# Bias rows in the routing, keys ahead of queries, and new orders in attention, in a fused cross-attention and mixture-of-experts kernel

## The reference, cut to what matters

```
x = x + attention(layernorm(x), ctx, ctx)        # scores / 4, causal mask, softmax, times values
h = layernorm(x)                                 # 1024 tokens x 256
logits = h @ router_weight.T + router_bias
top_val, top_idx = top_k(logits, 4); scores = softmax(top_val) placed at top_idx, else 0
gate, up = split(h @ gate_up_proj[e] + gate_up_bias[e])      # min(gate, 7), clip(up, -7, 7)
out_e = ((up + 1) * gate * sigmoid(1.702 * gate)) @ down_proj[e] + down_bias[e]
x = x + sum_e scores[:, e] * out_e
```

## Time and profile before

| what | us |
|---|---|
| median of 3 runs | 311.38 |
| the profiled execution | 311.51 |
| its span, first to last instruction | 309.8 |
| attention, to the last copy of `o_t` (L706) | 0 to 106.9 |
| routing, to the first L1535 | 106.9 to 134.7 |
| block loop, to the end of the last L1535 | 134.7 to 286.6 |
| last stage | 286.6 to 309.8 |
| PE busy in the span | 268.6 (87%) |
| DVE busy | 183.5 (59%) |
| ACT, POOL busy | 159.1, 159.0 (51% each) |

### The profile page before, as it was taken

One profiled execution on the slowest core, in us unless ns is written; L12 is line 12 of the kernel. 1 busy time (PEld: TensorE's weight loads), 2 busy tenths in 40 slices (PEclk: granted clock), 3 DMA queues, 4 the chain that ended last, 5 costly groups with the idle time before them and its releaser, 6 DMA issues.

```text
span 309.8 us, 5662 instructions
## 1 busy us (share of the span) xinstructions
PE 268.6 (87%) x1517; PEld 175.4 (57%) x1523; DVE 183.5 (59%) x479; ACT 159.1 (51%) x361; POOL 159.0 (51%) x225
## 2 busy tenths in 40 slices
PE   7796897699799625779999989999998989998994
PEld 7764565376577414435655655666655656555673
DVE  3897746944868787535535545555544546654495
ACT  3334655335465437646557556676755755654200
POOL 6871815712535777253566656666557565553000
PEclk9799999959999955899999999999999999999759
DMA  7605050043059999154232222222232222331693
GB/s 249 231 3 190 19 204 3 1 156 119 2 194 355 413 412 372 43 159 167 81 104 74 87 72 88 88 90 88 75 85 87 85 91 72 82 83 47 234 329 135
DMA packets 26494, 42.35 MB, mean 137 GB/s; under 512 B 2688, under 2 KB 19168, under 8 KB 26208
## 3 DMA queue, kind: packets, MB, share of 16 engines
q1 hardware_dynamic: 21776, 29.27, 26.3%
q0 software_dynamic: 4416, 12.45, 13.2%
q10 hardware_dynamic: 272, 0.26, 0.3%
HBM read 29.66 MB, written 12.26 MB: 135 GB/s over the span
## 4 chain that ended last, share of the span: by engine, by line
PE 71%; DVE 12%; issue 4%; ACT 4%; DMA 3%; another core or an unknown queue 2%; POOL 1%; SPq 1%; ACTq 0%; DVEq 0%
PE ps L1535 27%; PE ps L1554 13%; DVE neg_max L897 6%; PE ps L1266 5%; PE ps L1544 4%; PE ps L1582 3%; PE ps L1518 3%; PE ps L1342 3%; PE ps L1318 2%; PE ps L1285 2%; PE ps L1569 2%; DMA br_sb<-n_L_ffn_router_bias_dram 2%; PE ps L1371 1%; DVE x_tok L929 1%
## 5 line engine op out<-in xcount | busy, mean ns | idle before, releaser
L1535 PE MATMUL ps<-w_all,q_norm 128*128 x188 | 90.4, 603 | 5.1 <-issue 2.6
L648 POOL DMA_INDIRECT pair_rows<-y_ext,slot_row x45 | 45.5, 1010 | 51.9 <-ACT y_ext L830 38.9
L1174 DVE TENSOR_SCALAR v_aug<-ps 128x256 f32<-128x256 f32 x47 | 20.0, 425 | 69.0 <-PE ps L1535 49.0
L642 POOL DMA_INDIRECT ctx_tok<-y_rows,slot_tok x47 | 46.0, 979 | 21.3 <-issue 14.0
L1535 PEld LDWEIGHTS ps<-w_all,q_norm 128*128 128x128 f32 x188 | 32.0, 190 | 32.0 <-issue 31.8
L1554 PEld LDWEIGHTS ps<-w_all,o_t 128*128 128x128 f32 x188 | 35.3, 190 | 25.8 <-issue 23.3
L1554 PE MATMUL ps<-w_all,o_t 128*128 x188 | 48.6, 381 | 1.1 <-ACT o_t L821 1.1
L557 POOL TENSOR_SCALAR_AFFINE_SELECT w_all<-w_all 128x256 f32<-128x256 f32 (+1 forms) x48 | 23.1, 500 | 41.6 <-ACT w_all L698 40.8
L816 ACT ACTIVATE v_aug<-v_aug 128x256 f32<-128x256 f32 x47 | 19.6, 417 | 46.1 <-DVE v_aug L1174 39.2
L698 ACT ACTIVATE w_all<-ps 128x512 f32<-128x512 f32 x48 | 25.7, 599 | 24.1 <-PE ps L1318 24.1
L897 DVE TENSOR_REDUCE neg_max<-ps 128x2 f32<-128x512 f32 (+1 forms) x48 | 30.5, 685 | 8.0 <-PE ps L1291 5.5
(11 more groups left out here) (161 smaller groups left out, 389.0 us busy)
## 6 DMA issues: line engine op xcount, KB each, us to landing
w_all<-_L_ffn_gate_up_proj_dram SPq DMA_DIRECT2D x16, 512.0 KB, 5.8
w_all<-in_L_ffn_down_proj_dram SPq DMA_DIRECT2D x16, 256.0 KB, 6.5
pair_rows<-zeros SPq DMA_DIRECT2D x4, 1024.0 KB, 4.5
bias_all<-n_gate_up_proj_bias_dram SPq DMA_DIRECT2D x2, 2048.0 KB, 12.4
w_all<-pair_rows SPq DMA_DIRECT2D x8, 512.0 KB, 6.6
x_tok<-in_x_dram SPq DMA_DIRECT2D x4, 256.0 KB, 4.4
out_dram<-x_tok SPq DMA_DIRECT2D x4, 256.0 KB, 2.1
ctx_tok<-in_ctx_dram SPq DMA_DIRECT2D x3, 256.0 KB, 5.3
```

The costliest lines, as they stand in the source:

```text
L642: pool.indirect_dma_start(out=xg[:, i % XG, :], out_offset=None, in_=y_dram[:, :], in_offset=bass.IndirectOffsetOnAxis(ap=slot_tok[:, i:i ...
L648: pool.indirect_dma_start(out=pair_dram[:, :], out_offset=bass.IndirectOffsetOnAxis(ap=slot_row[:, i:i + 1], axis=0), in_=o_sb[:, i % O_RI ...
L1535: mm = pe.matmul(o, x_t[:, i % 3, k, :], w_all[:, bass.ds(e, 1), k * 2 * F:(k + 1) * 2 * F].rearrange("p a n -> p (a n)"), start=False, st ...
```

## The change

- In attention, `stack_low` and `dup` do the keys before they wait for the queries.
- M of batch 0's first half comes before its last four X steps, and `slot(0)` and `slot(1)` are written anew.
- The statistics of batches 2 and 3 move from the start into `slot(0)`, their powers behind masks; `x1_rows(0)` moves from the middle of `slot(1)` to behind M(2, 1), and `tokens(0)` from the end of `slot(1)` into `slot(2)`.
- PE turns the router's weights just before M(0, 0).
- The routing scores are turned in two halves. The bias rows are made in the routing, in banks 0, 1, 4 and 5, and DVE adds them onto `x_tok` (x1) there: batches 0 and 1 between `router_scores(2)` and `places(2)`, 2 and 3 behind `slot_tokens`. `open_banks` and the eight fill matmuls are gone, and four stand ahead of the last two batches' bias rows.
- In the last stage no bias rows are made. `planes_of` also adds x1 onto the planes, and `last_sum` opens its banks itself.

```diff
 def slot(b):
+    if b == 0:
+        order = [("T", new, (0, 1, 2)), ("S", b, (0,)), ("M", b, (1,)), ("S", b, (1,)),
+                 ("T", new, (3, 4, 5)), ("S", b, (2,)), ("T", new, (6,)), ("X", new, (0, 1)), ("T", new, (7,)),
+                 ("X", new, (2, 3)), ("S", b, (3,)), ("X", new, (4, 5)), ("S", b, (4,)), ("X", new, (6, 7)),
+                 ("V", b, (0,)), ("M", new, (0,)), ("X", new, (8, 9)), ("V", b, (1,)), ("X", new, (10, 11)),
+                 ("S", b, (5,)), ("V", b, (2, 3)), ("M", new, (1,))]
+    if b == 1:
+        order = [("T", new, (0, 1, 2)), ("V", old, (4,)), ("T", new, (3, 4, 5)), ("V", old, (5,)),
+                 ("S", b, (0,)), ("V", old, (6,)), ("T", new, (6,)), ("V", old, (7,)),
+                 ("X", new, (0, 1)), ("S", b, (1,)), ("X", new, (2, 3)), ("S", b, (2,)),
+                 ("X", new, (4, 5)), ("S", b, (3,)), ("O", old, (0, 1)), ("T", new, (7,)), ("S", b, (4,)),
+                 ("X", new, (6, 7)), ("V", b, (0,)), ("M", new, (0,)), ("X", new, (8, 9)),
+                 ("V", b, (1,)), ("X", new, (10, 11)), ("S", b, (5,)), ("V", b, (2, 3)),
+                 ("M", new, (1,))]
...
 first = (("T", (0, 1, 2, 3, 4, 5)), ("X", (0, 1)), ("T", (6,)), ("X", (2, 3)), ("T", (7,)),
-         ("X", (4, 5, 6, 7, 8, 9, 10, 11)), ("M", (0,)))
+         ("X", (4, 5, 6, 7)), ("M", (0,)), ("X", (8, 9, 10, 11)))
...
 def stack_low(eng, b):
-    eng.wait_ge(stack_hi, 2 * b + 2)
-    eng.wait_ge(q_norm_ready, TB * (b + 1))
+    eng.wait_ge(stack_hi, 2 * b + 1)
     eng.tensor_tensor(ks[:, :, 48:64], src_k, ks[:, :, 0:16].bitcast(F32), ALU.subtract).then_inc(stack_lo, 1)
+    eng.wait_ge(stack_hi, 2 * b + 2)
+    eng.wait_ge(q_norm_ready, TB * (b + 1))
     eng.tensor_tensor(qs[:, :, 16:32], src_q, qs[:, :, 0:16].bitcast(F32), ALU.subtract).then_inc(stack_lo, 1)
...
 def row_bank(b):
-    return (0, 1, 0, 5)[b]
+    return (0, 1, 4, 5)[b]
...
 # POOL
-            for b in range(1, B):
-                rsqrt(b, 0)
+            rsqrt(1, 0)
...
                     select(u + 1)
-                    if n == (1 if b == B - 1 else 4) and b >= 1:
-                        rsqrt(b - 1, 1)
+                    if b == 0 and n in (1, 4):
+                        rsqrt(2 + n // 4, 0)
+                    if b == 2 and n == 0:
+                        rsqrt(0, 1)
+                    if b == 2 and n == 4:
+                        rsqrt(1, 1)
+                    if b == 3 and n == 1:
+                        rsqrt(2, 1)
...
 # DVE
+            def b_rows(b):
+                dve.wait_ge(b_rows_full, b + 1)
+                rows = ps[:, row_bank(b), :].rearrange("p (t d) -> p t d", t=TB)
+                dve.tensor_tensor(x_tok[:, TB * b:TB * b + TB, :], rows, x_tok[:, TB * b:TB * b + TB, :], ALU.add
+                                  ).then_inc(b_rows_ready, 1)
...
                 elif kind == "X":
                     row_max(b, n)
-                    if b >= 2 and n == 5:
-                        x1_rows(b - 2)
-                    if b >= 2 and n == 7:
-                        variance(b - 2, 1)
+                    if b == 3 and n == 5:
+                        x1_rows(1)
+                    if b == 3 and n == 7:
+                        variance(1, 1)
                 elif kind == "M":
                     max_rows_t(b, n)
                     if b == 0 and n == 1:
                         small_weights()
-                        block_tables()
+                        dve.wait_ge(x_in[2], 16)
+                        row_stats(4)
+                        row_stats(5)
+                        variance(2, 0)
+                    if b == 2 and n == 1:
+                        x1_rows(0)
+                        variance(0, 1)
...
-                    if n == 5 and 1 <= b < B - 1:
-                        tokens(b - 1)
+                    if b == 0 and n == 3:
+                        dve.wait_ge(x_in[3], 16)
+                        row_stats(6)
+                        row_stats(7)
+                        variance(3, 0)
+                    if b == 0 and n == 5:
+                        block_tables()
+                    if b == 2 and n == 2:
+                        tokens(0)
+                    if b == 2 and n == 5:
+                        tokens(1)
...
             router_scores(2)
+            b_rows(0)
+            b_rows(1)
             places(2)
...
             slot_tokens()
+            b_rows(2)
+            b_rows(3)
...
 def planes_of(tiles):
+                step(dve.tensor_tensor(x_tok[:, tiles, :], planes[:, tiles, 0, :], x_tok[:, tiles, :], ALU.add))
...
 # PE
+            scores_t(0)
+            down_rows(0)
             tokens_t(B - 1)
             router_logits(2, NT - 2)
             router_logits(2, NT - 1)
+            down_rows(1)
             ranks(2)
             counts()
-            open_banks()
             slots(0)
             slots(1)
             places()
             slots(2)
             block_slots()
-            scores_t()
+            scores_t(1)
+            fill(5, 4)
+            down_rows(2)
+            down_rows(3)
...
-            fill(4, 8)
...
-            down_rows(0)
             down(NB - 2)
-            down_rows(1)
             h_turn(NB - 1)
-            down_rows(2)
-            down_rows(3)
             last_sum(NS)
```

More of the change, by code:

```diff
@@ L187, in xattn_moe @@
         bias_put = sem("bias_put")
-        banks_open = sem("banks_open")
         w_early = sem("w_early")
@@ L775, in _ @@
             spread_lows(0, 0)
+            scores_turned(0)
             spread_lows(0, 4)
@@ L1106, in _ @@
             variance(0, 0)
-            for b in range(1, B):
-                dve.wait_ge(x_in[b], 16)
-                for t in range(TB):
-                    row_stats(TB * b + t)
-                if b == 1:
-                    queries(0)
-                    stack_low(dve, 0)
-            for b in range(1, B):
-                variance(b, 0)
+            dve.wait_ge(x_in[1], 16)
+            row_stats(2)
+            row_stats(3)
+            queries(0)
+            stack_low(dve, 0)
+            variance(1, 0)
             for kind, b, n in steps:
@@ L1231, in out_rows @@
                 dve.wait_ge(last_full, j + 1)
-                dve.tensor_tensor(x_tok[:, tiles, :], planes[:, tiles, 0, :],
+                dve.tensor_tensor(x_tok[:, tiles, :], x_tok[:, tiles, :],
                                   ps[:, (2, 3, 1, 0)[j], :].rearrange("p (t d) -> p t d", t=TB)[:, tiles.start - 2 * j:tiles.stop - 2 * j, :],
                                   ALU.add).then_inc(sum_ready, tiles.stop - tiles.start)
-            for j in range(4):
-                dve.wait_ge(b_rows_full, j + 1)
-                rows = ps[:, (2, 3, 1, 0)[j], :].rearrange("p (t d) -> p t d", t=TB)
-                dve.tensor_tensor(rows, rows, x_tok[:, 2 * j:2 * j + 2, :], ALU.add).then_inc(b_rows_ready, 1)
+            dve.wait_ge(b_rows_ready, B)
             for tiles in (slice(0, 2), slice(2, 4), slice(4, 6), slice(6, 7), slice(7, 8)):
                 planes_of(tiles)
+            settle()
             for j in range(4):
@@ L1452, in _, with router_t @@
                 pe.transpose(ps[:, SCORE[0], 0:P], ident[:, :], ident[:, :])
-            pe.wait_ge(small_in, 32)
-            for k in range(KD):
-                tr = pe.transpose(ps[:, 7, k * E:(k + 1) * E], wr_sb[:, k * P:(k + 1) * P], ident[0:E, 0:E])
-            tr.then_inc(small_t, 1)
+            def router_t():
+                pe.wait_ge(small_in, 32)
+                for k in range(KD):
+                    tr = pe.transpose(ps[:, 7, k * E:(k + 1) * E], wr_sb[:, k * P:(k + 1) * P], ident[0:E, 0:E])
+                tr.then_inc(small_t, 1)
             for kind, b, n in steps:
@@ L1464, in _ @@
                 elif kind == "M":
+                    if b == 0 and n == 0:
+                        router_t()
                     maxima_t(b, n)
@@ L1557, in down @@
                 mm.then_inc(dn_done, 1)
-            def down_rows(j):
-                bank = (2, 3, 1, 0)[j]
-                if j == 0:
-                    pe.wait_ge(b_down_in, 16)
-                    pe.wait_ge(score_t_ready, 2)
-                    pe.wait_ge(xt_ready, NB)
-                if j >= 2:
-                    pe.wait_ge(u_ready, NB - 3 + j)
-                for t in range(TB):
-                    mm = pe.matmul(ps[:, bank, t * D:(t + 1) * D], score_t[0:E, TB * j + t, :], b_down[0:E, :],
-                                   start=(t == 0), stop=True, skip_group_check=True)
-                mm.then_inc(b_rows_full, 1)
             def last_sum(i):
```

60 lines of the change are left out of this document (33 added, 27 removed).

## The result

Measured: 313.27 us in the median of 20 executions (310.66 to 315.63), beside 310.01 for the kernel before, 20 executions (307.55 to 316.91). The ratio is 1.0102, 95% interval 1.0071 to 1.0134: about 3 us slower. The forecast was 309.0, 0.8% faster. The time lies in the range; the sign is wrong.

A forecast was written before the change was run, and what follows sets the result against it. PE waits on DVE's maxima in attention, DVE has no gap in the routing, and PE's and DVE's sums run side by side last. -0.5 - 4.7 + 0 + 0.8 + 1.35 + 0.7 = -2.35 gave 309.0 us, range 303.5 to 313.8.

The forecast's parts named there:

- Step 1: Start: one copy of 1.03 us and the router's turns (0.3) leave the chain; T at about 8.9, 1.4 earlier.
- Step 2: slot(0): first S at about 23, X(1, 0) at 28.5 behind statistics and queries; slot ends 0.5 us earlier.
- rival (d): slot(0): POOL's power holds up DVE, X(1, 0) at 32.9, +3.6 in place of -0.5, 313.1 us; chance 0.13.
- Rival (a): slot(0): the early start is kept as DVE's gaps close, -3.6 instead of -0.5, 306.0 us; chance 0.15.
- Step 3: slot(1): x1_rows(0) leaves the maxima, 2.9 earlier, and no fall of the clock, 1.8 less; -4.7 us.
- Step 4: slot(2): tokens(0) ahead of attn_out puts two normalisations in DVE's chain of maxima; +0.8 us.
- Step 5: Routing: DVE's bias additions ahead of places(2) delay the end, +1.35 us; open_banks worth nothing, last bias rows hidden.
- Step 6: Last stage: PE's sums start 4.6 earlier, but DVE's new addition on the planes sets the end; +0.7 us.
- (c): Attention or routing: PE falls to 1.2 GHz or reaches 2.4 GHz late without open_banks and fills, 311.7 us; chance 0.21.

The follow-up runs named there:

- attention half: Kernel before with only the new attention orders, keys ahead of queries and statistics one by one; bias rows, opened banks and fills as before: 302.0 beside 306.02, ratio 0.9889.
- the four extra ones: Two filling matmuls behind each of the first two turns of gathered rows, added to the new attention orders with slot(0)'s filling: 307.0 us, 0.9891 to the kernel before.
- the two halves: Kernel before with only the attention changes, ratio 0.9889; and with only the bias-row move, no opened banks or fill of eight, third addition in last stage, ratio 1.0191.
- the last chip: Changed kernel with slot(0)'s filling, 312.26 us, against new attention orders with slot(0)'s filling and four matmuls behind the first gathered-row turns, 307.0: ratio 1.0189.
- without the third addition: Changed kernel with x1 copied by DVE into the last sums' four banks ahead of the planes, instead of added in planes_of: 305.75, ratio 1.0053 to the kernel before.
- the late additions: Changed kernel with DVE's additions of the bias rows of batches 0 and 1 moved from ahead of places(2) to behind slot_tokens(): ratio 1.0052 to the kernel before.

## Why the prediction was wrong

**Step 1.** T at 9.17 for 8.9, S(0, 0) at 21.61 for 23. The 24 turns took 2.81: the clock stayed, so the start was quicker than priced. With the old start the 24 turns took 4.50 and 4.19 where the clock fell, and 2.84 in the two profiles where it stayed. In all 13 profiles with the new start it stayed; whether the new start is the reason, 13 beside two of four don't settle.

**Step 2.** X(1, 0) at 27.06 for 28.5; rival (d) fell with it. The slot ended at 41.61, 0.67 later instead of 0.5 earlier, by a fall of the clock; at full clock it ends at 38.84, against 38.98 and 39.37 for the old orders at full clock from the start on. So the orders are worth 0.1 to 0.5, the clock up to 2.8, and the fall is a matter of chance in both (old orders: in one of four profiles). Rival (a), the start kept, was never seen: 1.0068 for start and `slot(0)` alone.

**Step 3.** The mechanism was right, the clock between 50 and 60 too; -3.6 for -4.7. `x1_rows(0)` took 0.74 for both additions, cost 0 as taken. The masks beside it paid, two in 2.07 us where two such took 1.28 at 25.75 in the attention half; V then waited 0.31 for POOL. By the exclusion rule of the Trainium skill (SBUF — State Buffer, section "SBUF: two separate sides") one of them has to wait: 0.79 longer masks beside 0.74 of additions agrees. But it was POOL that waited (the long mask is recorded from 63.55 to 65.03, the additions from 63.80; spans on POOL are rough, so which began first is not shown), and the term did not go to its upper end. The two rows, of DVE and of POOL:

```profile
63.80 0.74 DVE L948 TENSOR_TENSOR x_tok<-x_tok,score_t 128x256 f32<-128x256 f32 x2
...
62.97 2.07 POOL L569 TENSOR_SCALAR_AFFINE_SELECT w_all<-w_all 128x512 f32<-128x512 f32 x2 [2.55 <-ACT w_all L715]
```

**Step 4.** 0 for +0.8: `slot(2)` took 22.04 beside 22.06. But the first 2.2 us of the old one ran at 1.2 GHz (to 68.4), and lifting them was booked in Step 3. The two are better read together: -3.6 for -3.9, nearly right.

**Step 5 is the one that failed.** Its +1.35 is right for what it counts: the first gather came 24.46 behind the last V for 23.14, +1.32. Two statements beside it are wrong. "`open_banks` is worth nothing: PE waits for DVE right behind it" leaves out, with the fill of eight, work on no path that PE's clock hung on: taken away or moved (with the four extra ones), it is worth 2.6 us (1.0084). What `open_banks` gives by itself was not measured. And "the last bias rows lie in the wait for the gathered rows": at 1.2 GHz scores, filling and rows take 6.4 us from 126.16, and the turn, possible at about 130.8 (3.2 behind the gather, as before), comes at 132.53. The cover was priced in one clock and stood in the other. By the marks of the first two profiles Steps 1 to 4 gave -3.05 for -4.4, Step 6 took 1.05 for 0.7, and what Step 5 put at 1.35 took 2.22 to the first gate and up matmul and 1.80 more to the fifth block. By time the move (Steps 5 and 6) costs 5.8 us in place of 2.05.

**Step 6.** The mechanism was right (DVE from the second or third pair on, PE done by 300, outputs back to back), the size low: +1.05 in the first pair of profiles, +1.5 between the two halves and +1.4 on the last chip, for +0.7; without the third addition 1.5 us come back.

**The rivals.** What came is the mechanism of (c), with a chance of 0.21, in both its places: in attention (in `slot(0)`, not `slot(2)`) and in the routing. Its price was low: 311.7 stood for 6.2 us at the lower level, and there were 10.2 in `slot(0)` and as many more than before in the routing (27.3 for 17.1). That (d)'s 313.1 lies beside the measured 313.27 is luck: its X(1, 0) at 32.9 came at 27.06. The sentence of the Trainium skill that stood beside it (TensorE: Matmul & The Clock Gate, Part 1), that the lower clock is the default and only activity lifts it, should have outweighed the row that showed PE waiting behind `open_banks`: the row tells what the matmuls delay, not what they keep up. That nobody waited for them shows only that they cost nothing, not that they bring nothing.

**What stays open.** How the 5.8 us divide exactly: clock in the routing (0.8%), additions ahead of `places(2)` (0.5%) and third addition (0.5%) make 1.8 of 1.9%, but each is uncertain by 0.4 to 0.5%, and the first two overlap, since the late additions also let the clock rise. What `open_banks` is worth alone. And how much of Steps 1 and 2 is a loss.

## What to carry to other kernels

Before calling an edit free because other work hides it, look at the granted clock of the stretch that is to hide it: cover at 2.4 GHz is only half a cover at 1.2 (the same eight bias matmuls took 1.99 and 3.78 us). Matmuls for which nothing waits can be what keeps the engine at its upper level; price their removal by what runs next, at the lower one. And work moved off PE's last stage onto DVE's routing has to be weighed on the chain that it lands in.

## Not expected of the hardware

The same instructions at the same times to 0.1 us, and then the clock falls in one execution and not in another: in `slot(0)`, where PE was busy for 8.0 of 10 us, it fell in five of seven profiles, at different times from 28.6 on. On one chip 28 executions of the kernel before went from 302.7 us at a mean granted clock of 0.949 to 312.7 at 0.912: time and clock go together there (correlation -0.95; -0.59 to -0.86 on the four other chips). With filling in the gaps (9.35 of 10) twelve executions on another chip lay within 299.5 to 303.3, where the kernel before spread from 302.1 to 309.3. But six executions of the attention half without the filling lay within 300.3 to 303.2 on a third chip, so that the narrower spread is not shown to be the filling's.

The last stage stayed between 22.4 and 23.2 us in every profile without the third addition, whether DVE or PE summed the last tiles. The eight plane transfers are very even: in all 17 profiles the last landed 14.2 to 14.5 us behind the first issue, at either clock of PE. Behind that landing came 6.6 to 7.3 us of DVE's or PE's sums and the output without the third addition, 8.4 with it.
